# A token table, an attention layer and two expert banks on one core: GpSimd's mixings spaced out, six tiles fetched on their own, three masked copies moved into attention's first steps

## The reference, cut to what matters

```python
scaled = num_value.astype(jnp.float32) / 1000.0
sin_table = jnp.sin(scaled[:, None] * freqs[None, :])
table = jnp.where(is_num[:, None], sin_table, weight)
h = table[x]                                       # (128, 128, 128)

# attention on layernorm(h): 8 heads of 64, sequences of 128
dots = jnp.einsum('bhid,bhjd->bhij', q, k) * scale[None, :, None, None]
dots = jnp.where(eye, jnp.float32(MASK_VAL), dots)
dots = jnp.einsum('bhij,hg->bgij', dots, mix_pre)
attn = jnp.einsum('bhij,hg->bgij', softmax(dots), mix_post)
h = h + attn_times_v @ Wout + bout

# feed-forward on layernorm(h): a shared one, and two banks of 8 experts with top-1 routing
h = h + gelu(x2 @ Ws1 + bs1) @ Ws2 + bs2 + bank_sp(x2) + bank_fq(x2)
```

## Time and profile before

| | us |
|---|---|
| median of three runs | 1513.22 |
| lowest and highest of them | 1505.02, 1519.65 |
| profiled execution, its own time | 1516.47 |
| its span in the trace | 1514.7 |
| TensorE (PE) busy | 1472.9 |
| ScalarE (ACT) busy | 1141.7 |
| VectorE (DVE) busy | 1046.2 |
| GpSimd (POOL) busy | 958.3 |

### The profile page before, as it was taken

One profiled execution on the slowest core, in us unless ns is written; L12 is line 12 of the kernel. 1 busy time (PEld: TensorE's weight loads), 2 busy tenths in 40 slices (PEclk: granted clock), 3 DMA queues, 4 the chain that ended last, 5 costly groups with the idle time before them and its releaser, 6 DMA issues. The chain is left out here.

```text
span 1514.7 us, 33790 instructions
## 1 busy us (share of the span) xinstructions
PE 1472.9 (97%) x11128; PEld 1363.5 (90%) x11128; DVE 1046.2 (69%) x2785; ACT 1141.7 (75%) x3445; POOL 958.3 (63%) x1041
## 2 busy tenths in 40 slices
PE   5889999999999999999999999999999999999999
PEld 2479999999999999999999999988999999999999
DVE  7887778787877887887787888774344333356665
ACT  5589888888888888888888888875555555555555
POOL 8075567888788788878878887675677666510000
PEclk8899999999999999999999999999999999999999
DMA  7324411211211111111111111012343234456664
GB/s 240 142 75 154 157 38 53 67 46 42 60 38 39 46 51 36 35 55 35 35 41 51 34 36 52 25 41 72 80 121 106 70 71 109 120 159 188 185 189 145
DMA packets 171502, 126.47 MB, mean 83 GB/s; under 512 B 30309, under 2 KB 154959, under 8 KB 171330
## 3 DMA queue, kind: packets, MB, share of 16 engines
q1 hardware_dynamic: 153794, 104.15, 22.9%
q0 software_dynamic: 17536, 20.17, 4.7%
HBM read 61.64 MB, written 78.66 MB: 93 GB/s over the span
## 5 line engine op out<-in xcount | busy, mean ns | idle before, releaser
L1148 ACT ACTIVATE expd<-masked,nmax 128x128 f32<-128x128 f32 x1024 | 395.8, 393 | 0.2 <-DVE nmax L1296 0.2
L916 POOL TENSOR_TENSOR prob<-expd,rtotal 128x1024 f32<-128x1024 f32 x128 | 243.1, 1900 | 127.4 <-DVE rtotal L1266 125.9
L1285 DVE COPY_PREDICATED masked<-off_diag,ps_s 128x1024 f32<-128x1024 int32 x128 | 175.1, 1368 | 143.1 <-PE ps_s L1046 143.1
L1086 PE MATMUL ps_o<-u,probT 128*128 128x128 f32 x2048 | 249.2, 275 | 0.0
L1086 PEld LDWEIGHTS ps_o<-u,probT 128*128 128x128 f32 x2048 | 239.2, 192 | 0.0
L1148 ACT ACTIVATION_READ_ACCUMULATOR expd<-masked,nmax 128x1 f32 x1024 | 196.7, 192 | 0.0
L1157 ACT ACTIVATE u<-ps_ut 128x1024 f32<-128x1024 f32 x128 | 131.4, 1027 | 64.6 <-PE ps_ut L1097 64.6
L1233 DVE TENSOR_TENSOR w_lo<-ps_w,w_hi 128x512 fp32r<-128x512 f32 x256 | 164.5, 682 | 2.1 <-ACT w_hi L1181 2.1
L1172 ACT ACTIVATE probT<-ps_ut 128x1024 f32<-128x1024 f32 x128 | 131.5, 1027 | 45.2 <-PE ps_ut L1054 38.8
L1181 ACT ACTIVATE w_hi<-ps_w 128x512 fp32r<-128x512 f32 x256 | 146.3, 596 | 16.8 <-PE ps_w L1072 10.6
L1070 PE MATMUL ps_w<-xT_hi,M_hi 128*128 128x256 f32 x512 | 155.1, 303 | 2.7 <-DVE xT_lo L1227 2.2
(11 more groups left out here) (247 smaller groups left out, 3848.7 us busy)
## 6 DMA issues: line engine op xcount, KB each, us to landing
turned<-x2T SPq DMA_DIRECT2D x32, 256.0 KB, 2.2
answers_sp<-zeros SPq DMA_DIRECT2D x16, 512.0 KB
answers_fq<-zeros SPq DMA_DIRECT2D x16, 512.0 KB
xT<-turned SPq DMA_DIRECT2D x56, 128.0 KB, 2.5
sh_back<-answers_sp SPq DMA_DIRECT2D x56, 128.0 KB, 2.3
sh_back<-answers_fq SPq DMA_DIRECT2D x56, 128.0 KB, 2.6
out<-res SPq DMA_DIRECT2D x56, 128.0 KB, 2.2
h_sb<-in_L_tok_weight SPq DMA_DIRECT2D x12, 512.0 KB, 5.6
```

The costliest lines, as they stand in the source:

```text
L916: nc.gpsimd.tensor_tensor(prob[k % 2][:, :].rearrange("p (g j) -> p g j", g=H), expd[k % 2][:, :].rearrange("p (g j) -> p g j", g=H), rtot ...
L1086: mm = nc.tensor.matmul(ps_o[:, 0:D], probT[k % 2][:, g * N:(g + 1) * N], u[k % 2][:, g * D:(g + 1) * D], start=(g == 0), stop=(g == H - 1))
L1148: ins = nc.scalar.activation(expd[(k - 1) % 2][:, g * N:(g + 1) * N], masked[(k - 1) % 2][:, g * N:(g + 1) * N], ACT.Exp, bias=nmax[(k - 1 ...
L1285: nc.vector.copy_predicated(masked[k % 2][:, :].rearrange("p (g j) -> p g j", g=H), off_diag[:, :].unsqueeze(1).to_broadcast([P, H, N]), p ...
```

## The change

- `OWN` goes from 4 to 6: GpSimd gathers six row tiles and six numbers; the last chunk is as wide as the others; statistics and deviations of six tiles are made in setup.
- Each mixing waits for a count of masked copies: `mix(c)` for `done` >= min(c + 2, 8).
- GpSimd fills both `masked` buffers, ScalarE none.
- TensorE's products start one place later (place 6), the last stands behind the loop; `M_hi` is made at place 10.
- `halves` for the own numbers stands before `reduce(5)`, no longer behind it.
- In attention the masked copies of late chunks 2 and 3 move behind the row maxima of step 0, that of late chunk 4 behind those of step 1. Tiles 4 and 5 are normalized at the end of step 0, turned by TensorE in step 1 (before, step 2). The gathers behind `s_late` are those of tiles 6 and 7 alone; `first_stats(4, 2)` and `first_deviations(0)` go; the residuals of tiles 4 and 5 come with the first four.

```diff
-OWN = 4
+OWN = 6
@@ setup, GpSimd
             for c in range(2 * HC):
+                pool.wait_ge(S["done"], min(c + 2, ON_TIME))
                 mix(c)
-            nc.gpsimd.tensor_copy(masked[1][:, :]...
+            for k in range(2):
+                nc.gpsimd.tensor_copy(masked[k][:, :]...
@@ setup, ScalarE
-                if c == 4:
-                    act.wait_ge(S["coef_out"], 2)
-                    prefill(0)
-                if c == 9:
+                if c == 10:
                     act.wait_ge(S["M"], 2)
@@ setup, TensorE
-                if 5 <= c:
+                if 6 <= c:
                     for half in range(2):
-                        product((c - 5) // HC, (c - 5) % HC, half)
+                        product((c - 6) // HC, (c - 6) % HC, half)
+            for half in range(2):
+                product(1, HC - 1, half)
@@ setup, VectorE
             for c in range(CHUNKS):
-                reduce(c)
                 if c == 5:
                     dve.wait_ge(S["numbers0"], 16 * OWN)
                     halves(slice(CHUNKS - 1, CHUNKS), VX - VC * (CHUNKS - 1))
+                reduce(c)
@@ attention
+        LATE_ROWS_AT = {0: (2, 3), 1: (4,)}
-        RESID_BEHIND = {12: (4, 5), 14: (6, 7)}
+        RESID_BEHIND = {14: (6, 7)}
@@ attention, GpSimd
-                if k == -1:
-                    first_deviations(0, S["first_stat"], S["first_rstd"])
@@ attention, TensorE
-                if k == 2:
-                    turn_x(4, k)
-                elif k % 2 and k not in (1, 3) and live(i, k + 3):
+                if k % 2 and k != 3 and live(i, k + 3):
                     turn_x(k + 3, k)
@@ attention, VectorE
+                for n in LATE_ROWS_AT.get(k, ()):
+                    if n == LATES - 1:
+                        dve.wait_ge(S["late_sine"], 1)
+                    late_rows(n)
-                if k == 1:
-                    first_stats(4, 2, S["first_stat"])
-            late_rows(2)
             low_w(0, 2)
             low_w(0, 3)
             low_x(1)
-            late_rows(3)
-            dve.wait_ge(S["late_sine"], 1)
-            late_rows(4)
```

More of the change, by code:

```diff
@@ L930, in step @@
                         pool.wait_ge(s_late, 16 * LATES)
[L931 removed]
+                    if t % 4 == 0 or t == OWN:
+                        q0 = t // 4 * 4
                         for b in range(4):
[L933 to L934 removed]
+                            need(pool, s_got[(q0 + b) % 8], landed(i, q0 - 8 + b))
+                        link(nc.gpsimd.tensor_copy(gi[(t // 4) % 2][:, :], ids[:, q0:q0 + 4]))
                     need(pool, S["x_made"], group(i, t - 8) + 1)
@@ L1183, in step @@
                                              ACT.Copy).then_inc(S["w_hi"], 1)
-                if k % 2 and k != 1 and live(i, k + 3):
+                if k % 2 and live(i, k + 3):
                     high_x(k + 3)
@@ L1326, in step @@
                         link.inc(nc.vector.tensor_copy(n2[:, :, 1], rstd[a][:, 4:8]))
-                if k % 2 == 0 and k >= 2 and live(i, k + 4):
-                    need(dve, S["rstd"], quad(i, k) + 1)
+                if k % 2 == 0 and k >= 0 and live(i, k + 4):
+                    if k + 4 >= OWN:
+                        need(dve, S["rstd"], quad(i, k) + 1)
                     normalize(k + 4)
```

33 lines of the change are left out of this document (11 added, 22 removed).

## The result

| | before | changed |
|---|---|---|
| median of 20 runs each, us | 1513.03 | 1519.48 |
| lowest and highest | 1505.02, 1519.65 | 1516.10, 1521.21 |
| profiled execution, its span | 1516.47, 1514.7 | 1519.61, 1517.9 |
| PE, DVE, ACT, POOL busy | 1472.9, 1046.2, 1141.7, 958.3 | 1474.3, 1032.4, 1142.0, 964.4 |

The ratio is 1.0042, 95% interval 1.0023 to 1.0061: the changed kernel is slower, by 0.4%. The forecast was 1.0 us faster; it had the sign wrong. One thing stands out in the 20 runs of each. Those of the changed kernel lie within 5.1 us. Those of before lie in two groups, nine from 1505.0 to 1508.7 and eleven from 1512.8 to 1519.7, with nothing between. The profiled execution of before belongs to the second.

The account below looks back on a forecast made before the run. TensorE is busy all the time from scores(6) on, so the start of scores(6) sets the time: -7.9 us in setup, +6.9 in attention, sum -1.0, median 1513.2 to 1512.2 (profiled 1516.5 to 1515.5); range 1503 to 1520.

Parts of the forecast that it names:

- gain of 7.9 us: Setup: attention begins at 53.5 instead of 61.4, 7.9 us earlier.
- (1): Setup: two more row gathers push GpSimd by 2.5 us; TensorE's coefficients begin at 13.8, the formerly stalled copy at 22.4.
- (2): Setup: own-number gathers begin at 15.1, the sixth lands at 26.6; `halves`, `reduce(5)` and the masked copy end at 29.7.
- Step (3): Setup: each masked copy releases one mixing; a chunk takes 3.24 us, the fourth further copy ends at 42.7.
- the rival of the low clock: Setup: TensorE stays at 1.2 GHz, a place costs 4.6 us, attention begins at 65.5; +11.0 us, 1524.2; chance 0.10.
- The stall: Setup: one masked copy takes 16.55 us instead of 1.28 beside the mixings; spacing them removes these 15.3 us of VectorE.
- VectorE, once second, doesn't get in: Setup: when GpSimd reads SBUF first, VectorE can't get in between instructions that follow each other closely.
- Attention's chain to tile 7's statistics: Attention: late copy 4, table and gathers complete tile 7's statistics 32.2 us after the start, against 25.3; 6.9 given back.
- 22.5 us to the mark, no slack: Attention: from tile 7's statistics to the start of scores(6), the mark, it takes 22.5 us, with no slack found.
- the uncured stall: Setup: spacing doesn't cure the stall, setup keeps its length and the 6.9 us are lost in full, 1520.1; chance 0.06.
- the surviving gain: Attention: slack or an earlier table lets the later steps keep the whole 7.9 us, 1505.3; chance 0.20.
- The three lower ends of the sum: Gathers landing in 2.6 (-1.5), chunks of 2.6 (-2.6), full clock in step 1 (-1.3); told as -6.4 together.

Follow-up runs that it names:

- e4: The kernel before, unchanged, run and profiled once more: median 1515.8 us, ratio 0.9997.
- e5: The kernel before with one more wait, the first mixing held until reduce(4) has ended: median 1507.2 us, ratio 0.9959.
- e6: The kernel before with the spacing of the mixings alone, products a place later and both fills on GpSimd: median 1504.6 us, ratio 0.9944.
- e2: The changed kernel with TensorE's turning of tiles 4 and 5 behind the quarters of `w` in step 1: median 1518.6 us, ratio 1.0015.
- e1: The changed kernel with SyncE's fills of the banks' rows two steps later: median 1518.8 us, ratio 1.0026.
- e3: The changed kernel with late copies 2, 3 and 4 back ahead of step 0: median 1512.9 us, ratio 0.9977.
- e7: The changed kernel with late copies 2, 3 and 4 back ahead of step 0 and SyncE's fills two steps later: median 1510.5 us, ratio 0.9984.
- e8: The same kernel as e1, run once more: median 1517.3 us, ratio 1.0024.
- e9: The kernel e6 with late copies 2, 3 and 4 moved behind the row maxima of steps 0 and 1: median 1516.1 us, ratio 1.0012.

## Why the prediction was wrong, point by point

**The base.** The sum was made against one profiled execution, and its gain of 7.9 us was the removal of a stall that 11 of 20 runs of before had and 9 hadn't. I then put the shift on the median of three, 1513.2, of runs at 1505.0, 1513.2 and 1519.7, and called their distance scatter. It was the one sign in the material that the stall is an outcome and not a cost (e4, e5). Against the faster group the spacing could win little: e6 began attention 3.5 us earlier than e4 and 1.6 earlier than e5; against the stalled profile 11.2. The sum made for the profiled execution, 1515.5, should have been told as it was: 4.1 below the 1519.6 that came. The median missed by 7.3 (1512.2 for 1519.5): these 4.1, and 3.3 from the base.

**Setup (predicted start 53.5, measured 56.74).** The steps that failed are (1) and (2), GpSimd's way to the own numbers, and by one term that the sum put at nothing: VectorE's masked copies hold GpSimd up too. I had used the exclusion in one direction only. The select of `head_of` at 13.23 began 0.07 inside a masked copy and took 1.67 for 0.60, so GpSimd was 3.7 late at `off_diag` where I had 2.5, and the number gathers began at 16.37 instead of 15.1; the fifth began inside the next copy (21.03) and took 1.73 for 0.95, ending 0.79 behind it. It is no accident of one execution: 21 gathers of setup, in 15 of the 16 profiles, began inside a masked copy, and each ended 0.78 to 0.80 behind it. The last gather's landing, 5.5 from its issue, was as read. So `halves` came at 28.93, not at 26.6, and the copy ended at 31.86, not at 29.7: 2.2. The coefficients, 1.15 later than in the sum, were hidden behind that wait. Step (3): four places took 14.1, not 13.0. Three were 3.13 to 3.16 for my 3.24; one was 4.7, because TensorE's second product took 3.78, and the angles behind it came 2.25 us late. That is the rival of the low clock in a small dose: one place, 1.5 us longer, where it had put 1.4 for a place. It isn't in every execution: e2 has it too (3.78, attention at 55.9), while e1, e3, e7 and e8, with the same setup, have 1.98 there and begin at 55.1 to 55.5. From there on 10.75 for my 10.8, though the last at the barrier wasn't VectorE but TensorE's warming matmuls.

**The stall (predicted gone): right.** That the two engines exclude each other was right too, for the masked copies, which read two arrays. The six own statistics, which read one, took 1.26 from 46.03 on beside a mixing (46.07), 0.21 each; with GpSimd idle four took 0.87 in the kernel before. "VectorE, once second, doesn't get in" was right for one of two outcomes: where a copy was under way when the mixings began, each VectorE instruction waits for one mixing. I had set the rule of the Trainium skill (SBUF — State Buffer, section on the two separate sides), by which whoever starts first has the port "for the whole instruction", against the trace. e4 and e5 agree with it (1.82 us for a small instruction, 1.63 for a copy), the first profile doesn't: both are to be had from the same code.

**Attention's chain to tile 7's statistics (predicted 32.2 after its start, measured 31.5): right**, with late copy 4 at 23.8 for 24.4, the table at 26.5 for 27.2, TensorE idle 3.65 for 3.6. Of the low clock behind it I had the full price in the sum; the record gives 0.82 for 74 to 81 and 0.63 for 85 to 92, and e2 prices the order at 1.9 for 2.1.

**"22.5 us to the mark, no slack": failed.** It measured 25.3. No slack was right; that the stretch is a constant was not. SyncE's first fill waits for the sixth scores, tile 12's gather for the probabilities of tile 2. Both stand in the stretch, and when the steps moved against the gathers, the fill came 0.26 behind the gather instead of 2.0, and the gather took 5.3 us instead of 2.6. e8 prices it: way 56.8 to 54.1, 2.7 of the 2.8 us. I had followed GpSimd, VectorE and TensorE there, and no DMA that another engine issues.

Together: 3.2 in setup, 2.8 behind tile 7's statistics, less 0.7, make 5.3: scores(6) at 113.54 for the predicted 108.2. Of the rivals, the uncured stall fell with the first profile after; the surviving gain fell with e3 and e9; the low clock had the right point of decision ("at 54.5 or later") and only that one place of its mechanism. That rival also called the first product's 3.46 in the earlier trace rows the low clock; the record reads 1.00 there (22 to 26), and only the pace speaks for it (see the end). The three lower ends of the sum add up to -5.4, to -6.4 only with the forecast's own -1.0. The range held the time, with 0.5 us to spare; that is its width and not the forecast.

## What to carry to other kernels

A time of before that comes in two groups is a finding: profile more than one execution and ask of which group each is, before a stall in one of them is sold as a gain. Where two engines share a way into memory, the order in which they meet can decide between waiting for one instruction and for all of them; a wait that lets the short one in first cost nothing that could be measured and was enough here (e5). And such an exclusion has two directions: whoever prices what one engine loses by it asks what the other loses. A copy on which a chain of put, landing and gather hangs stays in front of work that only its own engine needs, and when steps move, the DMAs that other queues issue on step counts move too.

## What the runs showed of the hardware that I had not expected

The granted clock in the record doesn't tell all. In setup of the changed kernel, where the product at 34.49 took 3.78 instead of 1.98, it reads 1.00, while weight loads of one size took 0.34 there and 0.19 at 39.76 (stretches with TensorE's part alone: length, busy, clock, DMA, GB/s; the second is of the kernel before; then weight loads of the changed kernel):

```profile
35.00:37.00 2.00, 2.00 (x3) 1.00 1.03 422
39.00:42.70 3.70, 3.70 (x5) 0.50 0.40 163
```

```profile
35.51 0.34 PEld L594 LDWEIGHTS ps_m<-mixed,wkT 128*128 128x128 f32 x1 [0.52 <-issue]
39.76 0.19 PEld L594 LDWEIGHTS ps_m<-mixed,wkT 128*128 128x128 f32 x1 [0.24 <-issue]
```

The ratio, 1.8 to 1.9, is near that of the two levels, 1.2 and 2.4 GHz. And in the kernel before the product at 39.12 took 3.67, with weight loads of 0.34, in a stretch where the record does read 0.50. So I take 35 to 37 for the low level too; why the record doesn't show it is open.

A gather of one tile's rows is held up by a large fill that another queue issues just after it, as by one just ahead: 5.3 us with the fill 0.26 behind (changed), 4.8 with it 0.23 ahead (e2), 4.3 with it 0.86 ahead (e3), and 2.6 to 2.7 with it 1.9 or more behind (before, e4, e5, e6, e9).

And the indirect gathers that GpSimd issues wait for a masked copy of VectorE: one that began inside it ended 0.78 to 0.80 behind it, 21 times out of 21, whatever it would have taken alone (0.95).
